# One core, cross-attention and a routed expert stage: paced indirect transfers, an earlier routing of the last pairs, and a tail on two queues

## The reference

```python
x = x + xattn(layernorm(x), ctx, ctx)            # 32 x 128 tokens, 16 heads of 8, 77 keys
y = layernorm(x)
proj = y @ Wp.T
gate = l2norm(proj) @ l2norm(sim_matrix).T / temperature     # 8 experts
top_v, top_i = top_k(gate, 2);  p = softmax(top_v)
h  = gelu(y @ W1[e] + b1[e])                     # 128 -> 512, for both chosen experts
eo = h @ W2[e] + b2[e]                           # 512 -> 128
out = x + sum over the two choices of p * eo
```

## Time and profile before

| | before |
|---|---|
| median of 3 runs | 444.5 us (443.37 to 445.08) |
| the profiled execution's own time | 443.8 us |
| its span, first to last instruction | 442.0 us |
| PE, ACT, DVE, POOL busy | 81%, 64%, 70%, 61% |
| mean granted TensorE clock | 0.948 |
| attention and routing, to the first L891 | 258.8 us |
| expert stage, to the last L902 | 420.5 us |
| tail | 21.5 us |
| indirect transfers on POOL | 71 of L561 and 64 of L446 |

### The profile page before, as it was taken

One profiled execution on the slowest core, in us unless ns is written; L12 is line 12 of the kernel. 1 busy time (PEld: TensorE's weight loads), 2 busy tenths in 40 slices (PEclk: granted clock), 3 DMA queues, 4 the chain that ended last, 5 costly groups with the idle time before them and its releaser, 6 DMA issues.

```text
span 442.0 us, 13885 instructions
## 1 busy us (share of the span) xinstructions
PE 359.1 (81%) x3564; PEld 299.5 (68%) x3565; DVE 310.4 (70%) x970; ACT 284.6 (64%) x815; POOL 268.3 (61%) x427
## 2 busy tenths in 40 slices
PE   3869888988897889888977878949869999989900
PEld 2447766665675667566755768949769999989900
DVE  5257989888988898889878555635546555556872
ACT  3458887878787878777877465725436565656531
POOL 5623367767686778776863345565655655556673
PEclk9969999999999999999999599978989999999965
DMA  6900001101110101012000032222212222129463
GB/s 172 371 1 5 20 27 40 44 28 33 32 43 24 31 31 43 24 31 82 27 26 14 19 76 56 57 61 63 68 51 67 64 68 61 54 61 264 119 173 113
DMA packets 39052, 29.24 MB, mean 66 GB/s; under 512 B 5107, under 2 KB 34751, under 8 KB 39008
## 3 DMA queue, kind: packets, MB, share of 16 engines
q1 hardware_dynamic: 30592, 18.33, 14.5%
q0 software_dynamic: 4384, 8.60, 6.2%
q10 hardware_dynamic: 4032, 1.77, 1.4%
HBM read 17.53 MB, written 11.62 MB: 66 GB/s over the span
## 4 chain that ended last, share of the span: by engine, by line
PE 59%; DVE 19%; issue 10%; SPq 4%; another core or an unknown queue 2%; DVEq 2%; ACT 1%; DMA 1%; POOL 1%; ACTq 0%; POOLq 0%
PE ps_s L902 14%; PE ps_s L891 13%; PE ps_o L654 8%; PE ps_t L643 6%; PE ps_s L627 5%; DVE rows L1248 5%; DVE sums L1180 3%; SPq L346 3%; PE ps_o L662 2%; PE ps_o L724 2%; PE ps_s L617 2%; PE ps_x L674 2%; DVE pr L1174 2%; DVE cxT L1197 1%
## 5 line engine op out<-in xcount | busy, mean ns | idle before, releaser
L561 POOL DMA_INDIRECT results<-eo,didx x71 | 70.6, 995 | 64.6 <-issue 34.4
L446 POOL DMA_INDIRECT lists<-rows,slots x64 | 65.4, 1021 | 47.8 <-DVE slots L1313 34.1
L891 PE MATMUL ps_s<-xtT,w1c 128*128 128x128 f32 x568 | 78.8, 283 | 7.5 <-DVE xtT L1576 5.5
L948 ACT ACTIVATE pT<-ps_t 77x512 f32<-77x512 f32 x128 | 72.2, 589 | 19.2 <-PE ps_t L643 17.4
L891 PEld LDWEIGHTS ps_s<-xtT,w1c 128*128 128x128 f32 x568 | 70.6, 195 | 12.4 <-DVE xtT L1576 10.0
L902 PE MATMUL ps_s<-w2s,hT 128*128 x568 | 77.5, 281 | 0.6 <-ACT hT L1108 0.4
L643 PE MATMUL ps_t<-identf,pr 128*77 128x128 f32 x512 | 74.5, 286 | 0.0
L902 PEld LDWEIGHTS ps_s<-w2s,hT 128*128 128x128 f32 x568 | 70.4, 195 | 1.2 <-issue 1.0
L1108 ACT ACTIVATE hT<-h 128x512 f32<-128x512 f32 x71 | 44.7, 629 | 39.2 <-PE ps_s L902 25.4
L1104 ACT ACTIVATE w1c<-w1s 128x512 f32 x71 | 44.8, 631 | 34.3 <-PE ps_s L891 16.7
L643 PEld LDWEIGHTS ps_t<-identf,pr 128*77 128x77 f32 x512 | 61.7, 154 | 6.5 <-issue 4.1
(11 more groups left out here) (204 smaller groups left out, 607.6 us busy)
## 6 DMA issues: line engine op xcount, KB each, us to landing
xt<-lists SPq DMA_DIRECT2D x71, 66.0 KB
ys<-results SPq DMA_DIRECT2D x16, 256.0 KB, 4.5
xin<-in_x_dram SPq DMA_DIRECT2D x16, 128.0 KB, 2.2
w1s<-in_L_ffn_W_dram SPq DMA_DIRECT2D x1, 2048.0 KB, 10.0
out_dram<-x ACTq DMA_DIRECT2D x6, 256.0 KB
cin<-in_ctx_dram SPq DMA_DIRECT2D x16, 77.0 KB
results<-eo,didx POOLq DMA_INDIRECT x71
lists<-rows,slots POOLq DMA_INDIRECT x64
```

Of the source, the lines that this page charges most:

```text
L446: nc.gpsimd.indirect_dma_start(lists, bass.IndirectOffsetOnAxis(ap=slots[:, r, s * TOPK + k:s * TOPK + k + 1], axis=0), rows[:, r, s, k, : ...
L561: nc.gpsimd.indirect_dma_start(results, bass.IndirectOffsetOnAxis(ap=didx[:, r:r + 1], axis=0), eo[:, r, :], None, bounds_check=TOPK * NTO ...
L891: last = nc.tensor.matmul(ps_s[:, r, c * P:(c + 1) * P], w1c[:, r, c * P:(c + 1) * P], xtT[:, r, :], start=True, stop=True)
L948: nc.scalar.activation(pT[0:SK, g, :], ps_t[0:SK, g % 2, :], ACT.Copy).then_inc(E[f"t{g}_ready"], 1)
```

## The change

1. **Fill.** After each `give_back` transfer POOL writes zeros over a scratch tile of 448 numbers a partition and raises `paced`; the next `give_back` transfer waits for it. Scatters have no fill of their own.
2. **Pair 14** is routed in the steps (bound `NP - 1`; DVE and PE run a step 18, POOL a step 16). Its scatters leave the tiles.
3. **Pair 15** moves ahead: `second_norm` at -1, `turn` at 0, `gate` at 2, `gate_power` at 1, DVE at 3, 4, 5, 7, 8, `rank` at 7, scatters at 8 to 11. The second tables start at 9, one stage a tile; the loop starts at 27.
4. **Sums.** `EARLY` = 11: three more batches beside the last tiles, 8 on POOL in place of 9.
5. **Tail.** ACT waits for all returns, loads chunk 7 beside SP's chunk 6, stores chunks 0 to 2, then weighs 6 and 7. SP stores 3 to 7. `all_given` is raised by a no-op.
6. **Start.** The two small products of the similarity matrix go from `ps_x` at the end of `values` to a corner of `ps_s` one step later, and PE waits for each itself. `sum_most` also waits for `expA`; each scatter transfer is issued by a call of its own.

```diff
-    DRAINED = 20
+    DRAINED = 9
+    LOOPED = DRAINED + 18
-    EARLY = 8
+    EARLY = 11
+    LATER = 3
...
+        pace = sb("pace", [P, 448])
...
-            all_returned(N_TILES)
-            for c in range(PART // CH, NB // CH):
-                load_results(c)
-            for c in range(PART // CH, NB // CH):
+            all_returned(sp, N_TILES)
+            load_results(sp, PART // CH)
+            for c in range(LATER, NB // CH):
                 store(sp, c)
...
-                if has(J, -2, NP - 2):
-                    scatter(J - 2, m - 2, 1)
+                if has(J, -2, NP - 1):
+                    scatter(J - 2, m - 2, 1, 0)
+                if has(J, -2, NP - 1):
+                    scatter(J - 2, m - 2, 1, 1)
...
-            steps(pool, step, 0, 15, 4, 13)
+            steps(pool, step, 0, 16, 4, 13)
...
                 after_tile(pool, FE["eo_ready"], j)
+                after_tile(pool, FE["paced"], j - 1)
                 settled(pool)
                 nc.gpsimd.indirect_dma_start(results, bass.IndirectOffsetOnAxis(ap=didx[:, r:r + 1], axis=0),
                                              eo[:, r, :], None, bounds_check=TOPK * NTOK - 1, oob_is_err=False
                                              ).then_inc(returned[r], 16)
+                nc.gpsimd.memset(pace[:, :], 0.0).then_inc(FE["paced"], 1)
...
-                if j == 9:
+                if j == 1:
                     gate_power(NP - 1, NP - 1)
-                elif 10 <= j < 14:
-                    scatter(NP - 2, NP - 2, (j - 10) // TOPK, [(j - 10) % TOPK])
-                elif 21 <= j < 25:
-                    scatter(NP - 1, NP - 1, (j - 21) // TOPK, [(j - 21) % TOPK])
+                elif 8 <= j < 12:
+                    scatter(NP - 1, NP - 1, (j - 8) // TOPK, (j - 8) % TOPK)
...
-            nc.gpsimd.memset(warm[:, :], 0.0).then_inc(all_given, 1)
+            pool.nop(nofuse=True).then_inc(all_given, 1)
...
-            steps(pe, step, 1, 17, 6, 14)
+            steps(pe, step, 1, 18, 6, 14)
...
-                if j == 2:
+                if j == 0:
                     after(pe, E["x2_ready"], NP - 1)
                     turn(NP - 1, NP - 1)
-                elif j == 3:
-                    rank(NP - 2, NP - 2)
-                elif j == 6:
+                elif j == 2:
                     after(pe, E["rk_ready"], NP - 2)
                     gate(NP - 1)
-                elif j == 15:
+                elif j == 7:
+                    after(pe, E["dots_ready"], NP - 1)
                     rank(NP - 1, NP - 1)
...
-            for c in range(PART // CH):
+            all_returned(act, N_TILES)
+            for c in range(PART // CH + 1, NB // CH):
+                load_results(act, c)
+            for c in range(LATER):
                 store(act, c)
...
-                elif DRAINED <= j < DRAINED + 7:
-                    for stage in range((j - DRAINED) * 2, (j - DRAINED) * 2 + 2):
-                        tables(1, stage)
+                elif DRAINED <= j < DRAINED + 14:
+                    tables(1, j - DRAINED)
```

More of the change, by code:

```diff
@@ L250, in xattn_moe_kernel @@
         returned = [sem(f"returned{r}") for r in range(FRING)]
-        fnames = "xtT_done xtT_ready didx_ready w1c_ready up_done h_ready act_ready down_done eo_ready".split()
+        fnames = "xtT_done xtT_ready didx_ready w1c_ready up_done h_ready act_ready down_done eo_ready paced".split()
         FE = {n: sem(n) for n in fnames}
@@ L259, in after_y, with all_returned, load_results @@
             eng.wait_ge(y_loaded[c], 16 * TOPK)
+        res = results.rearrange("(k c t p) d -> c k p t d", k=TOPK, t=CH, p=P)
+        def all_returned(eng, tiles):
+            for r in range(FRING):
+                eng.wait_ge(returned[r], len(range(r, tiles, FRING)) * 16)
+        def load_results(eng, c):
+            for k in range(TOPK):
+                eng.dma_start(ys[:, c, k, :, :], res[c, k]).then_inc(y_loaded[c], 16)
         def store(eng, c):
@@ L372, in _ @@
             rows_are_there(1, NB)
-            res = results.rearrange("(k c t p) d -> c k p t d", k=TOPK, t=CH, p=P)
-            def all_returned(tiles):
-                for r in range(FRING):
-                    sp.wait_ge(returned[r], len(range(r, tiles, FRING)) * 16)
-            def load_results(c):
-                for k in range(TOPK):
-                    sp.dma_start(ys[:, c, k, :, :], res[c, k]).then_inc(y_loaded[c], 16)
             late = PART_DONE + FRING + 1
             steps(sp, load_tile, early, late - 1, early, late - 1, FRING)
-            all_returned(PART_DONE)
+            all_returned(sp, PART_DONE)
             for j in range(late, max(N_TILES, late + PART // CH)):
@@ L437, in _, with scatter @@
             pool.wait_ge(headmask4_ready, 1)
-            def scatter(J, m, s, ks=range(TOPK)):
+            def scatter(J, m, s, k):
                 r = m % RING
@@ L444, in scatter @@
                 settled(pool)
-                for k in ks:
-                    nc.gpsimd.indirect_dma_start(lists, bass.IndirectOffsetOnAxis(ap=slots[:, r, s * TOPK + k:s * TOPK + k + 1], axis=0),
-                                                 rows[:, r, s, k, :], None).then_inc(scattered[r], 16)
+                nc.gpsimd.indirect_dma_start(lists, bass.IndirectOffsetOnAxis(ap=slots[:, r, s * TOPK + k:s * TOPK + k + 1], axis=0),
+                                             rows[:, r, s, k, :], None).then_inc(scattered[r], 16)
             def destinations(J, m):
@@ L803, in step @@
                     keys(J, m)
+                if known(J - 1) and J - 1 == 1:
+                    pe.wait_ge(simt_copied, 1)
+                if known(J - 1) and J - 1 == 2:
+                    pe.wait_ge(wgp_copied, 1)
                 if has(J, -1):
@@ L825, in step @@
                     turn_sums(J - 2)
+                if known(J - 3) and J - 3 == 0:
+                    pe.wait_ge(wgp_copied, 1)
                 if has(J, -3, NP - 1):
@@ L919, in between @@
                     count_rows(NP - 1, ps_x[:, 0:NE])
-                elif j == DRAINED + 8:
+                elif j == DRAINED + 15:
                     after(pe, E["xn2T_ready"], NP - 1)
                     tables(1)
-                elif j == DRAINED + 11:
+                elif j == LOOPED:
                     pe.wait_ge(tab_ready, 5)
-            steps(pe, tile, -2, N_TILES, DRAINED + 11, N_TILES - 3, FRING, between)
+            steps(pe, tile, -2, N_TILES, LOOPED, N_TILES - 3, FRING, between)
         @block.scalar
@@ L1110, in between @@
             def between(j):
-                if j == 4:
+                if j == 1:
                     turned(NP - 1)
-                elif j == 8:
+                elif j == 3:
                     gated(NP - 1, NP - 1)
-                elif j == DRAINED + 11:
+                elif j == LOOPED:
                     act.wait_ge(tab_ready, 5)
-            steps(act, tile, -2, N_TILES - 1, DRAINED + 11, N_TILES - 3, FRING, between)
+            steps(act, tile, -2, N_TILES - 1, LOOPED, N_TILES - 3, FRING, between)
             act.wait_ge(E["diff_ready"], NP)
@@ L1178, in sum_most @@
             def sum_most(J, m, s):
+                after_b(dve, E["expA"], J * 2 + s)
                 after_b(dve, E["exp2"], J * 2 + s)
@@ L1464, in step @@
                     tables(0, 0)
-                if has(J, -3, NP - 2):
+                if has(J, -3, NP - 1):
                     ranks(J - 3)
@@ L1531, in _ @@
             nc.vector.scalar_tensor_tensor(bo[:, :], bo_row[:, :], anyk[:, 2:3], ps_t[:, 0, 0:D], ALU.add, ALU.add).then_inc(bo_ready, 1)
-            steps(dve, step, 0, 17, 6, 13)
+            steps(dve, step, 0, 18, 6, 13)
             dve.wait_ge(tab_ready, 3)
@@ L1645, in _ @@
             for c in range(EARLY // CH, NB // CH):
-                mine = [b for b in range(c * CH, (c + 1) * CH) if not on_pool(b)]
+                mine = [b for b in range(c * CH, (c + 1) * CH) if b >= EARLY and not on_pool(b)]
                 after_y(dve, c)
```

112 lines of the change are left out of this document (49 added, 63 removed).

## The result

The changed kernel took 461.38 us (median of 4 runs, 459.59 to 464.71) against 444.79 for the kernel before in the same session (443.37 to 445.69): ratio 1.0385, 95% interval 1.0316 to 1.0453. It is slower by 16.6 us, where 427.5 was forecast and the range ended at 438. The profiled execution took 459.6, span 457.7.

What follows compares the result with a forecast made beforehand. PE's two products in the expert stage bound it, with some 22 us lost behind the first 8 tiles. 5.2 + 13.6 - 3.5 - 0.5 + 1.5 = 16.3 off 443.8 gave 427.5 us, range 421 to 438.

Steps and rivals of the forecast that it cites:

- the part on the fill: POOL's fill behind each transfer: cycle 1.38 becomes 1.79 to 1.85, wait on `paced` free, gain 5.2 us in the loop.
- third rival: POOL becomes the bound: DVE holds off the fill, cycle exceeds the tile's; 448.8 us at cycle 2.2, chance 0.08.
- The fill's length and the gain of spacing: In the loop: 448 numbers take 471 ns; transfers spaced about 1.8 free PE of late reports, gain 5.2 us.
- first rival: In the loop, spacing does not free PE and the remaining scatter group costs 8: 437.7 us, chance 0.14.
- the sum of 432.7: Forecast less the loop's 5.2 us, if by the skill's rule on SBUF ports spacing buys nothing.
- One group of scatters in place of two: In the tiles, losses of 16.6 us round two scatter groups become 3.0: gain 13.6, bounds 8 and 16.
- The start: First tiles: pair 14's routing delays the first product by 2.2; net -2.0, half clock -1.5, bounds 0 and -6.
- The half clock: First tiles: PE's pause brings half clock, three products costing 1 us each, half of it counted: -1.5 us.
- The tail: After the tiles: ACT weighs chunks 6 and 7 sooner, POOL ends 0.7 to 2.3 earlier; net gain 1.5 us.
- Sums beside the tiles: Last tiles: three more batches, 6 DVE instructions of 0.35, ask for chunk 0 earlier; cost 0.5, bounds 0 and 3.
- The sum: Whole kernel: gains and costs total 16.3 us, taken from the profiled execution's 443.8, forecast 427.5; chance 0.58.

Runs made afterwards that it cites:

- the wait two back: The changed kernel with two fill buffers in turn, transfer j waiting for the fill of tile j - 2 instead of j - 1: 432.59 us, ratio 0.9652.
- the kernel with the wait four back: The changed kernel with four fill buffers in turn, transfer j waiting for the fill of tile j - 4 instead of j - 1: 432.80 us, ratio 0.9595.
- the kernel with neither: The changed kernel without the fill and without its wait on `paced`, all else of the change kept: 443.81 us, ratio 0.9831.

## Why the prediction was wrong, point by point

**The step that failed** is in the part on the fill: "The wait on `paced` adds nothing: POOL runs in order and the fill of j - 1 is over by then." The fill is over by the time the transfer would start, and no fill was late. But it is not over by the time POOL's queue comes to the wait: with the wait two back the queue has passed it and made its move at 363.7, before the fill has begun. So what the wait costs is that the transfer's preparation of 0.74 us may not start before the fill ends: 0.60 us a transfer, a cycle of 2.39 in place of 1.79. I asked when the awaited work ends, and not what the queue would have done in the meantime. The trace of before held the answer: the move at 364.2 inside a transfer that ran from 363.6 to 364.6. With this wait POOL's own work sets the time of every transfer from the third on, and so the end. My own third rival had the price: its formula (275.6 + 70 c for the last transfer, less 2.3 from the tail) gives 442.9 for the last transfer and 462.1 us for the time at c = 2.39; measured were 438.96 (a scatter lengthens a distance by 0.6, not by 1.3, and the first transfer came 2.8 earlier, at 266.5) and 461.4. I gave it 0.08 because I had looked for a cause of a long cycle only in DVE holding off the fill. That cause did not occur: 71 fills took 487 ns in the mean. So the Trainium skill's lock between DVE and GpSimd (page "SBUF — State Buffer", section "Who interferes with whom") did not show in the fills, which are as long here as the forecast had them.

**The fill's length and the gain of spacing** were right. Forecast 471 ns and a cycle of 1.79 to 1.85; measured 487 ns and 1.79. Forecast 5.2 us in the loop; the kernel with the wait four back needs 51.19 where before needed 56.82, a gain of 5.6. The first rival (spacing does not free PE) falls by the same row. So does the sum of 432.7 that I set beside the forecast; that the kernels with the wait two and four tiles back have medians of 432.59 and 432.80 is chance, as their loop did win 5.6. The Trainium skill, same page, section "SBUF: two separate sides", has PE wait for no one's port, and I had said that the spacing then buys nothing. It bought 7.5 us against the kernel with neither; whether a port of SBUF has anything to do with it, no run here shows.

**One group of scatters in place of two** was forecast at 13.6, with 8 as the lower bound "if the group that is left costs as now". The lower bound was the answer: 64.21 became 56.32 with the wait four back, a gain of 7.9 (55.94 and 8.3 in the change itself). I had taken four pairs for four times a pair's cost in the loop (0.3 each). But these pairs stand 1.65 apart from each other, so it was a row of eight at 1.5 in the mean, and that stalls PE nearly as the row of five at 1.3 did. With a fill behind each scatter as well, and the scatters on every second tile, the window is 50.63, a gain of 13.6: the size was right for a change that spaces its scatters too.

**The start** was forecast at -3.5. From the start of the last projection's group to tile 0's first product it was 256.30 to 258.77 before, 2.47, and is 4.50 after, of which 2.62 idle of PE behind DVE:

```profile
251.92 0.68 PE L665 MATMUL ps_o<-wT,cxT 128*128 128x128 f32 x4 [1.78 <-DVE cxT L1208]
255.23 0.17 PE L683 MATMUL ps_x<-sel,tri 128*128 128x16 bf16 x1 [2.62 <-DVE selsum L1303]
```

So 2.0 late where I had 2.2; the thirteen kernels with pair 14 ahead of the tiles have 4.48 to 5.04 there, that is 2.0 to 2.6 late. The half clock came as well, 0.81 over the first 8 tiles (0.76 in a sibling), which is partly the 1.2 GHz level, and those tiles took 19.19 in place of 17.28. Together -3.9 against the trace of before. But the three kernels of the experiments that leave pair 14 where it was took 19.09 to 19.12 for these tiles too, with the start of before (2.47) and a granted clock of 0.84 to 0.87; against them the change's start costs 2.1. So the loss of 1.9 in the tiles cannot be put down to the pause that I named. That the first product of the change stood earlier, at 256.42, is the attention part's doing: its last projection started anywhere from 251.9 to 257.5 from kernel to kernel, and I know of no edit that moves it, so I count it to none. The clock may have a share in it: PE had a granted clock of 0.50 from 242.60 to 252.80 before, and of 1.00 over the same stretch in the change.

**The tail** was forecast at +1.5. From the last transfer's start to the end of the span it is 19.7 before and 18.8 after, 17.8 with the wait four back: a gain of 0.9 and 1.9, where the term had 2.3 before it took off 0.8 for the later transfers. Counted from the start of the last matmul, which takes the later transfers in, it is 21.8 before (L902 at 420.2) and 20.7 with the wait four back (L910 at 410.5): 1.1 beside the 1.5. ACT now weighs the late chunks once they land, and no longer behind DVE's sums, as the forecast had it (after; compare):

```profile
447.51 1.86 ACT L1137 ACTIVATE ys<-ys,p 128x128 f32<-128x128 f32 x6 [17.60 <-DMA ys<-results]
```

**Sums beside the tiles** had a cost of 0.5. Tiles 60 to 70 took 19.23 with the wait four back and 19.21 before, so it did not show.

**The sum.** With the wait two or four tiles back the ratio of 0.9652 or 0.9595, on 444.8, is 429.3 or 426.8 us, beside the 427.5 forecast. That nearness is partly luck: the group of scatters brought 5.7 us less than its term, and the kernel before, as run in those sessions, was up to 1.5% slower than the execution that my sum was made against (450.63 against 443.8), for reasons that I have no profile of. By their own medians, 432.59 and 432.80, those two kernels are 5 us above the forecast, which is about what the group of scatters fell short.

## What to carry to other kernels

A wait costs not only the time until its condition holds, but also the preparation that its queue would have done ahead. In front of an indirect transfer a wait for POOL's own newest instruction cost about 0.6 us a transfer wherever it was tried, and two buffers with a wait two steps back did the same duty for nothing. Ahead of `places` the same wait cost only 0.18; other engines were not tried. When pricing a wait, look in the trace of before at whether the queue's records (moves, semaphore records) of the next instruction lie inside the instruction that runs: if so, that overlap is what the wait can take away. And where an engine is close to the tile's period, work the sum for "this engine bounds everything" with a cycle put together instruction by instruction, gaps included, before giving it a small chance.

## What the runs showed of the hardware that I had not expected

- An indirect transfer of POOL starts no less than 0.74 us after its register move (71 transfers in each of 17 traces), and at just that distance where POOL has nothing else to do; 0.60 to 0.68 us of that comes into the open behind a wait for POOL's own newest instruction (2.39 against 1.79 with the same fill; 2.06 against 1.38 with no fill).
- In a row of close indirect transfers it seems to be the mean distance and not the shortest one that decides whether PE stalls: rows of alternately 1.35 and 1.65 (mean 1.5) stall PE for 6 to 7 us, rows of 1.29 and 2.04 (mean 1.67, the kernel that waits for its own `places`) did not, with no tile from 9 to 23 above 2.2. They did not leave it untouched: DVE's `eo` still started up to 1.6 us behind the end of its product (294.04 and 295.64). Over tiles 33 to 60 the lateness is 7.5 us at 1.38, 1.65 at 1.58, and gone at 1.79. "Late reports" is my name for DVE and ACT starting long after the end that the profile gives the product, and that end is modelled; whether the report or the product is late, no record tells. What the transfers and PE have in common stays open; no run was made on it.
- Adding 0.49 us of work to an engine on every tile made the kernel faster, by spacing what it issues: in the kernel before (0.9769), and in the change (0.9595 with the fill and the wait four back, 0.9831 with neither).
